# Rows and outputs of a graph attention layer taken from PSUM by ScalarE instead of VectorE, with the output bias summed on TensorE

## The reference, cut to what matters

```python
h = relu(layernorm(x))
D = abs(h[:, :, None, :] - h[:, None, :, :])
s = einsum('bijc,oc->bijo', D, W1) + b1               # 64 values for each pair
s = leaky((s - mean) / sqrt(var + eps) * g1 + be1)    # statistics over all pairs
s = einsum('bijo,uo->biju', s, W2)[..., 0] + b2
A = softmax(where(adj > 0, s, NEG))
y = einsum('bij,bjc->bic', A, h) @ Wg.T + bg
y = leaky(batchnorm(y) * gg + beg)                    # statistics over all nodes
x = x + concat(h, y) @ Wt.T + bt
# second layer: layernorm, a graph attention with a softmax over nodes, elu, residual
```

## Time and profile before

| | us |
|---|---|
| median of 3 runs | 1157.24 (1155.14 to 1157.57) |
| the profiled execution | 1156.38 |
| its span | 1154.6 |
| pass 1 | about 0 to 659 |
| pass 2 | about 663 to 1003 |
| tail | about 1003 to 1048 |
| layer 2 | about 1048 to 1155 |

### The profile page before, as it was taken

How to read it: one execution, slowest core, us unless ns; L and a number is a source line. 1 busy time by engine, 2 the same in 40 slices (tenths; PEclk the granted TensorE clock), 3 DMA queues, 4 the chain that set the end, 5 groups by cost and what they waited for, 6 DMA issues and landing times.

```text
span 1154.6 us, 17648 instructions
## 1 busy us (share of the span) xinstructions
PE 1054.3 (91%) x6470; PEld 473.9 (41%) x6470; DVE 1047.1 (91%) x1389; ACT 993.4 (86%) x1252; POOL 580.9 (50%) x332
## 2 busy tenths in 40 slices
PE   3999999999999999999999999999999999835997
PEld 1333333333333433333333452333333333335997
DVE  5999999999999999999999867999999999755887
ACT  4889998999999999999999889989899898703987
POOL 6587768767777877686777400111212221171330
PEclk9999999999999999999999989999999999976999
DMA  6444444444443444444444688999899999730012
GB/s 178 165 156 184 172 158 169 184 166 188 166 192 146 174 185 171 159 185 184 171 168 176 235 321 292 335 332 339 319 339 329 321 334 324 222 92 1 29 47 74
DMA packets 97269, 233.32 MB, mean 202 GB/s; under 512 B 8096, under 2 KB 44448, under 8 KB 97184
## 3 DMA queue, kind: packets, MB, share of 16 engines
q1 hardware_dynamic: 93040, 223.11, 53.2%
q0 software_dynamic: 2560, 8.39, 2.1%
q10 hardware_dynamic: 1584, 0.69, 0.3%
HBM read 124.43 MB, written 107.74 MB: 201 GB/s over the span
## 4 chain that ended last, share of the span: by engine, by line
PE 47%; DVE 37%; issue 7%; ACT 7%; DMA 1%; POOL 1%; ACTq 0%; DVEq 0%; POOLq 0%
PE psum L741 16%; DVE store L291 16%; PE psum L751 10%; PE psum L755 7%; DVE plain_st L1040 5%; DVE store L1055 4%; ACT store L567 3%; PE psum L932 1%; PE psum L916 1%; PE psum L933 1%; DVE early L1160 1%; PE psum L731 1%; PE psum L950 1%; PE psum L941 1%; PE psum L713 1%
## 5 line engine op out<-in xcount | busy, mean ns | idle before, releaser
L291 POOL TENSOR_TENSOR store<-h_ext 128x2048 f32<-128x2048 f32 (+1 forms) x96 | 386.6, 4029 | 119.5 <-PE psum L741 115.6
L741 PE MATMUL psum<-store,w1tt_sb 128*64 128x512 f32 x1792 | 421.1, 598 | 17.7 <-ACT store L567 17.5
L291 DVE TENSOR_TENSOR store<-psum,h_ext 128x2048 f32<-128x2048 f32 x160 | 364.1, 2275 | 0.7 <-ACT h_ext L537 0.7
L567 ACT ACTIVATE store<-store 128x2048 f32<-128x2048 f32 x160 | 305.1, 1932 | 6.2 <-POOL store L291 3.1
L644 ACT ACTIVATE store<-store,st 128x1024 f32<-128x1024 f32 x192 | 226.5, 1241 | 0.0
L741 PEld LDWEIGHTS psum<-store,w1tt_sb 128*64 128x64 f32 x1792 | 122.0, 136 | 252.8 <-issue 236.2
L751 PE MATMUL psum<-store,w_twice 128*64 128x512 f32 x768 | 200.6, 599 | 4.9 <-DVE early L1005 3.5
L291 DVE TENSOR_TENSOR store<-h_ext 128x2048 f32<-128x2048 f32 x64 | 146.2, 2285 | 17.9 <-PE psum L741 17.9
L1040 DVE BATCH_NORM_STATS2 plain_st<-store 128x6 f32<-128x512 f32 x256 | 160.6, 678 | 0.0
L755 PE MATMUL psum<-early 128*64 128x512 bf16 x1152 | 158.0, 380 | 0.0
L845 PE MATMUL psum<-store,w_rows 128*32 128x512 f32 x1024 | 134.3, 607 | 3.2 <-ACT store L644 3.2
(11 more groups left out here) (155 smaller groups left out, 1195.6 us busy)
## 6 DMA issues: line engine op xcount, KB each, us to landing
kept_products<-store SPq DMA_DIRECT2D x192, 512.0 KB, 2.7
store<-kept_products SPq DMA_DIRECT2D x192, 512.0 KB, 6.0
early<-score_skew POOLq DMA_DIRECT2D x16, 384.0 KB, 6.8
early<-adj SPq DMA_DIRECT2D x16, 256.0 KB, 3.6
early<-adj_t SPq DMA_DIRECT2D x16, 256.0 KB, 3.5
store<-x SPq DMA_DIRECT2D x16, 256.0 KB, 5.6
out<-early SPq DMA_DIRECT2D x16, 256.0 KB, 2.3
score_skew<-early POOLq DMA_DIRECT2D x16, 128.0 KB, 6.0
```

Source lines behind the costliest of these rows:

```text
L291: return engine.tensor_tensor(t[:, :, 0:steps, :], nodes.unsqueeze(2).broadcast_to([C, 2, steps, N]), windows(h_ext[:, 2 * c, :], STEP * m ...
L567: nc.scalar.activation(t, t, ACT.Abs).then_inc(abs_ready, 1)
L741: last = nc.tensor.matmul(t[MID * g:MID * g + MID, b, :], w1tt_sb[:, 0:MID], diff[slot][:, g, b * BANK:b * BANK + BANK], start=True, stop= ...
```

## The change

1. `take_rows` goes from DVE to ACT, at the same step (24).
2. `att_y` is split. ACT adds the bias and writes y (`y_to_nodes`, step 56). DVE keeps the statistics (`y_sums`, step 57). PE's waits for the bank go to the new semaphore `y_out`.
3. The bias `bt` goes into PE's sums. DVE splits it into three bf16 parts once in pass 1 (`split_bias`), and one bf16 matmul (`biases`) opens the PSUM bank of each output group. POOL's `x_and_bias` is gone.
4. ACT issues the 16 loads of x: eight ahead of its last activation, eight behind it. The write and read of the skewed scores of the last two quads go from POOL to SP.
5. `PRE` is 8 instead of 6, with new places for `outputs_of_x` and `fold_x`.
6. The three dumps of the statistics' sums in pass 1 go to other places in SBUF.

```diff
+        BY_POOL = NQ - 2
-        FOLD_AT = tuple(QCH * j + step for j in (NQ - 2, NQ - 1) for step in (SCORES, NORM, COPY))
-        MADE_AT = (264, 266, 270, 274, 277, 284)
+        FOLD_AT = [QCH * (NQ - 1) + TURN] * 2 + [QCH * (NQ - 2) + step for step in (SCORES + 1, NORM, COPY, Y_SUMS)] + \
+            [QCH * (NQ - 1) + step for step in (SCORES, NORM)]
+        MADE_AT = (257, 258, 266, 267, 270, 273, 277, 282)
...
+            def take_rows(j):
+                act.wait_ge(scored, PER * (j + 1))
+                if j > 0:
+                    act.wait_ge(dist_turned, j)
+                nc.scalar.activation(s_rows[:, :], score[j % 2], ACT.Identity, bias=B2).then_inc(rows_ready, 1)
+
+            def y_to_nodes(j):
+                act.wait_ge(out_mm, j + 1)
+                nc.scalar.activation(h_nat[:, quad(j), :], att[0], ACT.Identity, bias=BG).then_inc(y_out, 1)
...
+                if n == CHUNKS - 2:
+                    act.wait_ge(prod2_ready, NPLAIN)
+                    for q in range(8):
+                        load_x(q)
+                if n == CHUNKS - 1:
+                    act.wait_ge(scored, CHUNKS // 2)
+                    for q in range(8, NQ):
+                        load_x(q)
...
+            def biases(o):
+                nc.tensor.matmul(o, ones_bf[:, :], bt_rows3[:, :].unsqueeze(1).broadcast_to([128, QUAD, C]),
+                                 start=True, stop=False)
...
-                for s, step in ((s_masked, SCORES), (y_ready, Y)):
+                for s, step in ((s_masked, SCORES), (y_out, Y)):
...
+            def split_bias():
+                in_turn(nc.vector.tensor_scalar(bt_sb[:, :], bt_sb[:, :], -1.0, None, ALU.add))
+                for k in range(2):
+                    in_turn(nc.vector.tensor_copy(bt_high[:, k, :], bt_sb[:, :]))
+                    in_turn(nc.vector.tensor_tensor(bt_sb[:, :], bt_sb[:, :], bt_high[:, k, :], ALU.subtract))
+                nc.vector.tensor_copy(bt_rows3[0:1, :], bt_high[0:1, 0, :])
+                nc.vector.tensor_copy(bt_rows3[32:33, :], bt_high[32:33, 1, :])
+                nc.vector.tensor_copy(bt_rows3[64:65, :], bt_sb[64:65, :]).then_inc(bt_ready, 1)
...
-            def att_y(j):
-                dve.wait_ge(out_mm, j + 1)
-                y = h_nat[:, quad(j), :]
-                linked(nc.vector.tensor_scalar(y, att[0], BG, None, ALU.add))
-                nc.vector.bn_stats(bst[:, j, :], y.rearrange("p b n -> p (b n)")).then_inc(y_ready, 1)
+            def y_sums(j):
+                dve.wait_ge(y_out, j + 1)
+                nc.vector.bn_stats(bst[:, j, :], h_nat[:, quad(j), :].rearrange("p b n -> p (b n)")).then_inc(y_ready, 1)
```

More of the change, by code:

```diff
@@ L306, in mix_at, with skewed @@
             return EARLY_MIX + u if r < 2 and 0 <= u < NQ - EARLY_MIX else None
+        BY_POOL = NQ - 2
+        def skewed(j):
+            whole = skew_dram[j % 2]
+            return bass.AP(whole.tensor, whole.offset + 1, [[EXT + 1, N], [N * EXT, QUAD], [1, DIST]])
         def quad_at(n, step):
@@ L376, in load_kept, with store_skew, load_half @@
                 sp.dma_start(loaded[k % LRING], kept_dram[k, :, :]).then_inc(kept_in[k % LRING], 16)
[L378 to L385, removed]
+            def store_skew(j):
+                sp.wait_ge(turn_ready, j + 1)
+                sp.wait_ge(half_in, 16 * (j - 1))
+                sp.dma_start(skewed(j), s_turn[:, :, :]).then_inc(late_stored[j - BY_POOL], 16)
+            def load_half(j):
+                sp.wait_ge(late_stored[j - BY_POOL], 16)
+                sp.wait_ge(s_sum, j)
+                sp.dma_start(s_half[:, :, :], skew_dram[j % 2].rearrange("b (i j) -> i b j", j=EXT))\
+                  .then_inc(late_in[j - BY_POOL], 16)
             FIRST_LOADS = (LRING - 1) // len(KEPT) * PER + KEPT[(LRING - 1) % len(KEPT)]
-            for n in range(CHUNKS + TAIL + AHEAD):
-                if n < CHUNKS and n % PER in KEPT:
+            for n in range(CHUNKS):
+                if n % PER in KEPT:
                     load_kept(n)
@@ L395, in _ @@
                           .then_inc(skew_cleared[s], 16)
-                if n == CHUNKS + AHEAD - 1:
-                    for q in range(NQ):
-                        load_x(q)
+            for j in range(BY_POOL, NQ):
+                store_skew(j)
+                load_half(j)
             def store_out(j):
@@ L498, in _ @@
             for j in range(NQ):
[L499 to L504, removed]
+                if j < BY_POOL:
+                    store_skew(j)
+                    load_half(j)
                 sum_half(j)
@@ L507, in _ @@
                     mask_l1(j - 5)
-            for q in range(PRE, NQ):
-                x_and_bias(q)
             pool.wait_ge(bn2_var, 1)
@@ L597, in sums @@
                                                      (1, ACT.Identity, dict(scale=256.0)))):
-                    at = 4 * first + (1024 if k == 1 else 0)
-                    dump = (sums_dump[:, :] if k == 2 else tiles(28, 4))[:, at:at + 4 * (last - first)]
+                    dump = sums_dump[k][part][:, 0:4 * (last - first)]
                     done = nc.scalar.activation(dump, counted_part(of)[:, 4 * first:4 * last], how,
@@ L1181, in _ @@
                     again(n + LEAD_DIFF)
-                for step, do in ((Y, att_y), (EVAC, take_rows), (TURN, take_turned), (SCORES, att_scores),
+                for step, do in ((Y_SUMS, y_sums), (TURN, take_turned), (SCORES, att_scores),
                                  (NORM, att_norm), (COPY, att_copy)):
@@ L1186, in _ @@
                         do(j)
-                if n in FOLD_AT:
-                    fold_x(FOLD_AT.index(n))
+                for k in range(PRE):
+                    if n == FOLD_AT[k]:
+                        fold_x(k)
             done[0] = 0
```

78 lines of the change are left out of this document (47 added, 31 removed).

## The result

The changed kernel takes 1147.61 us (median of 4 runs, 1147.24 to 1149.4), the kernel before 1156.19 beside it: a ratio of 0.9924, 95% interval 0.9903 to 0.9945. That is faster by 0.76%, and 0.6 us from the forecast of 1147.0. The terms behind the sum did not all come out. One execution in this document ran at a lower granted clock and took 20 us more, the profiled one of light_work_behind_low (1163.54 us, clock 0.939); of that kernel only the times of the others are used.

The account below looks back on a forecast made before the run. It took DVE to set the pace of pass 2, with PE, ACT and transfers within 10%. Pass 2 -5, tail -5, layer 2 +0.2 and pass 1 +0.3 sum to -9.5 from 1156.38: 1147 predicted, range 1139 to 1152.

Parts of the forecast that it names:

- The loop of pass 2: Pass 2: waits between DVE and ACT through y, `y_sums`, `att_scores` and `exps` set a quad at 20.4 us, from 20.76.
- the loop does not bind: Rival, pass 2: `y_sums` finds y ready, ACT alone sets 19.7 us, 7 more gained, 1140; chance 0.11.
- The tail: From `exps` of quad 13 to the aggregation of y's statistics: 42.8 us instead of 47.8, so -5.
- Both ends meet: Tail: `att_sum` of quad 15 can start near 30.8 us, and its halves are there at 29 to 31.
- ACT issues faster: Rival, tail: eight x loads cost ACT 3.5 us instead of 6.7, quad 15 some 6 earlier, 1141; chance 0.18.
- slower: Rival, tail: ACT's 16 issues block, 15 us come onto the path, 1162; chance 0.07, half of it only to no change.
- Pass 1: Chunk 32: eight DVE operations of 128 columns, 0.2 us each, 1.6 in all, mostly hidden behind PE; +0.3.
- The cover: Pass 1: DVE, 37.28 us busy of 39.3, hides work of this size behind PE; without it the cost is 1.6.
- Layer 2: Layer 2: two quads save 1.8 us of half matmuls, eight bf16 bias matmuls add 2.0; +0.2.

Follow-up runs that it names:

- light_work_behind_low: The kernel of split_in_pass2 with eight unused statistics of 128 columns on DVE at the end of turn 32 of pass 1, behind `low`: 1143.04 us, ratio 0.989.
- sums_later: The changed kernel with y's statistics (`y_sums`) moved from step 57 to step 60, behind `take_turned` and `att_scores`: 1149.12 us, ratio 0.9947.
- x_from_sync: The changed kernel with the 16 loads of x issued by SP instead of ACT: 1139.82 us, ratio 0.9865.
- sums_next_quad: The changed kernel with y's statistics (`y_sums`) moved from step 57 to step 72, in turn 8 of the next quad: 1143.19 us, ratio 0.9899.
- split_in_pass2: The changed kernel with `split_bias` moved from chunk 32 of pass 1 to turn 4 of pass 2: 1143.11 us, ratio 0.9899.

## Why the prediction was right, and where it was not

**The loop of pass 2: right, in mechanism and size.** Predicted 20.4, measured 20.32. DVE idles 1.09 where 1.2 was put, ACT 0.58 where 0.7 was. y took 0.68 where the estimate from 512 and 1024 columns was 0.66. The formula of the Trainium skill, "ScalarE: Activation LUTs", section "What ACT_TABLE_LOAD costs", gave an estimate of 0.71, so the row lies between. The 11 quads gave 4.8, not 4.0, and the last period 0.1, not 0.3. The first quads gave more than the 0.5 put down: from the end of pass 1 to the store of quad 2 it took 90.7 (750.04 less 659.32) and now 89.3.

**The rival "the loop does not bind": it did not come, and was wrong as it was put.** It gave ACT's own 19.7 once `y_sums` finds its y ready. sums_later did that and stayed at 20.30, for the second loop has almost the same length. The prediction had seen one loop and said that nothing else was late. Only with both cut does ACT set the period, at 19.90.

**The tail: right, a little undersized.** -5 predicted, -6.2 measured. The row of quad 15 left ACT 16.7 behind the `exps` of quad 13 (1015.19 - 998.52), not 18.4, because the issues took 6.1 (0.39 + 5.71) and 5.7 and not 6.7 each (the first few of a batch took 0.37 to 0.53, most later ones 0.7 to 1.8, so the pause between the batches saved little); `att_sum` of quad 15 started 29.5 behind and not 30.8; from there it was 12.0 as predicted. "Both ends meet" was not so. POOL's sum of the last halves started at 1023.22:

```profile
1023.22 0.72 POOL L496 TENSOR_TENSOR early<-early 128x256 f32<-128x256 f32 x1 [21.75 <-DMA early<-score_skew]
```

It ended at 1023.94, 7.4 behind the masked rows (1015.93 + 0.62) and not 9 to 11, so the halves were ready 25.4 behind `exps`. What decided is the chain through y, scores and mix of quad 14, and that chain began late because of the issues. The rivals "ACT issues faster" (3.5) and "slower" (15 on the path) are both out. The prediction called the loads in ACT's queue the cost of the change and put 9.8 on the rows. In x_from_sync the rows leave ACT 7.8 sooner (1007.68 - 998.76 = 8.9 behind `exps`, not 16.7), and the tail as a whole is 9.5 shorter. The size of the tail is known to about 1 us only, by the scatter named with sums_next_quad, so -6.2 and -5 do not clearly differ.

The rival "ACT issues faster" had a rule of the Trainium skill beside it: by "DMA: Bandwidth & Descriptors", section "Issuing engines are not separate DMA queues", the sequencer's time to start a transfer is usually small beside the transfer. For one load of x the rows do not speak against it: the 16 took 11.8 us of ACT's queue, 0.74 each, and a load landed in a median of 5.2. What decided here is that 16 in a row add up, and that ACT had work behind them. The time of the 16 is nearly the same on SP and ACT. The issues of the changed kernel, on its page (KB each, median us to landing):

```profile
store<-x ACTq DMA_DIRECT2D x16, 256.0 KB, 5.2
```

**Pass 1: the step that failed.** "+0.3", from 1.6 us of work hidden behind PE. What was wrong in it is the duration. 0.2 each holds for operations that run alone, but one cast stood 4.0 us behind POOL's subtraction, so the whole took 6.3. The rows of the kernel before had shown such waits in the tail, where DVE operations of 0.69 took 5.00 and 2.14 beside POOL; the prediction reckoned with them there and not here. The cover was right: DVE had 2.0 us to spare in a window of 39.3, and the table shows 1.9 hidden, at whatever length. With the measured 6.3 in place of 1.6, the prediction's own working gives 6.3 - 1.9 = 4.4.

The Trainium skill, "SBUF — State Buffer", section "SBUF: two separate sides", states this: DVE and GpSimd share a port pair that one of them holds for a whole instruction, and it is asked for by a DVE operation in one of the fast modes that use two ports, or by one with two inputs in SBUF when GpSimd reads SBUF too. The rows agree: the cast 4.24 against 0.23, the subtraction `low` 3.71 against 0.41, while statistics of one input ran beside POOL at 0.60 each. In which mode the cast ran, no row shows.

**Layer 2: right in the sum.** +0.3 for +0.2. Its two terms, 1.8 saved and 2.0 added, were not measured apart.

That the total hit to 0.6 us is in part luck. Two misses cancel in part: pass 2 and the tail gave 12.5 where 10 were put, and pass 1 took 4.6 more than its term. The sum of the spans is -7.3 against -9.5, and the profiled execution took 1149.4 where the sum gave 1146.9; the median lies 1.8 below it, and the medians moved by 8.6. With `split_bias` in pass 2 the kernel stands at 1143, as split_in_pass2 shows.

## What to carry to other kernels

When work moves from one engine to another, draw every loop that passes through both queues, and the ones through their neighbours too. Here ACT had 19.7 us of work per quad, PE 19.4 and DVE 18.9; the second loop was as long as the first, and cutting one gave nothing. A DVE cast in SBUF, or an operation with two inputs in SBUF, must be placed by what POOL does at that moment, not by how long it is. What is then added to DVE costs what goes beyond the time that DVE has to spare at that place. Transfers belong on the queue of an engine that nobody waits for.

## What the runs showed of the hardware

- A DVE cast of 128 columns in SBUF takes 0.23 alone and 4.24 when it begins just behind the start of a POOL subtraction of 2048 columns (4.21); a subtraction of 256 columns with two inputs in SBUF takes 0.41 and 3.71. Statistics of 512 columns keep 0.60.
- 16 loads of 256 KB each hold the issuing queue for 11.8 us on ACT and 12.0 on SP, each in two batches of eight, and for 13.37 on SP in one batch. The transfer engines were busy in all three (a share of 0.80 to 1.01).
- A bias on 512 columns from PSUM takes ACT 0.68, and the next operation starts 0.57 later (808.84 and 809.41).
